# Attention blocks turned through HBM instead of sixteen small transfers, the normalisation moved from GpSimd to VectorE, and a new order of the work

## What is computed

```
x: (128, 128, 256) float32;  adj: (128, 128, 128) int32, 0 or 1, with 1 on the diagonal
nx = layernorm(x; ln1)
q, k, v = nx @ wq + bq, nx @ wk + bk, nx @ wv + bv          # 8 heads of 32
bias   = where(adj > 0, 0.1 * adj * adj, -inf)
attn   = softmax(q k^T / sqrt(32) + bias)                   # (128 graphs, 8 heads, 128, 128)
x1     = x + (attn v) @ wo + bo
out    = x1 + gelu(layernorm(x1; ln2) @ w1 + b1) @ w2 + b2  # hidden width 1024
```

## Time and profile before

| | |
|---|---|
| median of 3 runs | 1980.41 us (1977.6 to 1981.12) |
| the profiled execution | 1975.85 us, its span 1974.1 us |
| busy: TensorE / VectorE / ScalarE / GpSimd | 77% / 59% / 56% / 37% of the span |
| TensorE's mean granted clock | 0.889 |
| DMA moved | 113.29 MB, 57 GB/s on average |
| instructions | 35182 |

### The profile page before, as it was taken

The page is one execution under the profiler, slowest core; times in us unless marked ns, Lnnn a source line. Parts: engine busy times, 40 slices in busy tenths (PEclk is TensorE's granted clock), DMA queues, the critical chain, the costliest instruction groups (busy, mean ns, idle before and its releaser), DMA issues.

```text
span 1974.1 us, 35182 instructions
## 1 busy us (share of the span) xinstructions
PE 1528.4 (77%) x11580; PEld 1288.1 (65%) x11580; DVE 1161.4 (59%) x2130; ACT 1114.1 (56%) x3140; POOL 722.8 (37%) x552
## 2 busy tenths in 40 slices
PE   6468778788778788778788778788778788778777
PEld 5347667667666666667667666667667666666667
DVE  4466656566565566565566565566565566565553
ACT  3355555565555565655565555565555565655542
POOL 4244432244332344332344332344332344332320
PEclk8589888888899898988898898898898898898889
DMA  3222211222112222112222111222112222111110
GB/s 110 57 59 60 58 53 49 62 67 59 51 48 59 63 65 60 53 46 60 63 66 57 53 49 56 64 66 58 53 47 58 64 65 59 52 47 55 49 50 26
DMA packets 153413, 113.29 MB, mean 57 GB/s; under 512 B 36112, under 2 KB 153104, under 8 KB 153360
## 3 DMA queue, kind: packets, MB, share of 16 engines
q1 hardware_dynamic: 153360, 112.61, 20.2%
HBM read 28.58 MB, written 16.78 MB: 23 GB/s over the span
## 4 chain that ended last, share of the span: by engine, by line
SPq 62%; PE 13%; issue 10%; DVE 8%; DMA 3%; POOL 2%; ACT 1%; DVEq 0%; POOLq 0%; ACTq 0%
SPq L299 59%; PE work L354 4%; DMA probt<-wa_raw 3%; PE work L356 3%; PE work L355 3%; DVE wa_raw L793 2%; DVE hid_parts L886 2%; POOL rstd L982 2%; PE work L430 2%; PE area L410 2%; SPq L291 1%; DVE st L821 1%; DVE res L897 1%; SPq L282 1%; SPq L273 1%
## 5 line engine op out<-in xcount | busy, mean ns | idle before, releaser
L588 ACT ACTIVATE soft<-soft,nmax 128x128 f32<-128x128 f32 x1024 | 396.5, 392 | 5.5 <-DVE nmax L773 4.8
L979 POOL TENSOR_TENSOR ve<-mv,eps 128x4 f32<-128x4 f32 x64 | 12.9, 202 | 1038.5 <-DVE mv L830 922.9
L430 PE MATMUL work<-probt,vals 128*32 128x128 f32 x2048 | 108.2, 342 | 302.6 <-DMA probt<-wa_raw 302.5
L354 PE MATMUL work<-w_hi,hid_parts 128*128 128x256 f32 x1024 | 302.6, 296 | 4.0 <-DVE res L897 3.0
L994 POOL TENSOR_TENSOR soft<-soft,rinv 128x1024 f32<-128x1024 f32 x128 | 242.8, 1897 | 157.3 <-DVE rinv L783 157.3
L598 ACT ACTIVATE at_hi<-work 128x256 fp32r<-128x256 f32 x128 | 49.1, 383 | 441.5 <-PE work L430 441.5
L430 PEld LDWEIGHTS work<-probt,vals 128*32 128x32 f32 x2048 | 64.5, 130 | 353.4 <-issue 346.2
L355 PE MATMUL work<-w_lo,hid_parts 128*128 128x256 f32 x1024 | 291.2, 284 | 0.0
L356 PE MATMUL work<-w_hi,hid_parts 128*128 128x256 f32 x1024 | 290.7, 284 | 0.0
L802 DVE TENSOR_TENSOR at_lo<-work,at_hi 128x256 fp32r<-128x256 f32 x128 | 54.0, 422 | 361.1 <-ACT at_hi L598 360.9
L886 DVE TENSOR_TENSOR hid_parts<-late_memory,hid_parts 128x512 fp32r<-128x512 f32 x256 | 223.0, 892 | 69.3 <-ACT hid_parts L656 69.3
(11 more groups left out here) (90 smaller groups left out, 3724.2 us busy)
## 6 DMA issues: line engine op xcount, KB each, us to landing
probt<-wa_raw SPq DMA_DIRECT2D x2048, 32.0 KB, 1.9
xin<-in_x SPq DMA_DIRECT2D x32, 512.0 KB, 3.6
out<-res SPq DMA_DIRECT2D x128, 128.0 KB, 1.8
adj_in<-in_adj SPq DMA_DIRECT2D x32, 256.0 KB, 2.8
res<-in_L_gnn_w SPq DMA_DIRECT2D x1, 1024.0 KB, 10.3
late_memory<-in_L_gnn_w SPq DMA_DIRECT2D x1, 1024.0 KB, 11.9
wa_raw<-in_L_gnn_wq SPq DMA_DIRECT2D x1, 256.0 KB, 3.8
wa_raw<-in_L_gnn_wk SPq DMA_DIRECT2D x1, 256.0 KB, 6.1
```

The source lines that it names most:

```text
L354: pe.matmul(o, lhs_hi, rhs_hi, start=first, stop=False)
L430: mm = pe.matmul(mixed[g * HD:(g + 1) * HD, c * P:(c + 1) * P], vals[:, par, b, c * RPB + g, :], probt[:, b % 2, :, g * DC + c, :], start= ...
L588: a = act.activation(soft[:, b % 2, h, :], soft[:, b % 2, h, :], ACT.Exp, bias=nmax[:, b % 2, h:h + 1], accum_out=rsum[:, b % 2, h:h + 1])
```

## The change

`shuffle` is replaced. `send_blocks` writes a whole turned block (512 KB) to a scratch tensor in HBM in one transfer; `fetch_blocks` waits until that has landed and reads it back in four transfers of 128 KB each, every one to a quarter of the partitions. `normalise` goes from GpSimd to VectorE, with the same operands. The orders of all engines and the banks of `UNITS` are new: `down` 3 lies in the step of the others, `flip` "nt" opens the step of `up`, `mix` 0 lies at the end of the step before the other mixes.

```diff
-LAND = RPB * RPB * 16
+LAND = RPB * 16
-FIRST, EARLY, LATE = -2, 6, 2
+FIRST, EARLY, LATE = -2, 4, 2
+        moved = nc.dram_tensor("moved_blocks", (2, RPB, HD, RPB, BLK), F32, kind="Internal").ap()
...
-            def shuffle(step, off, b):
...
+            def send_blocks(step, off, b):
...
                 sp.wait_ge(blocks_ready, step.through(off, GB, b))
-                for i in range(RPB):
-                    for j in range(RPB):
-                        sp.dma_start(probt[j * HD:(j + 1) * HD, b % 2, i, :, :],
-                                     blocks[i * HD:(i + 1) * HD, b % 2, j, :, :]).then_inc(landed[b % 2], 16)
+                sp.dma_start(moved[b % 2].rearrange("i k j n -> (i k) (j n)"),
+                             blocks[:, b % 2, :, :, :].rearrange("p j h q -> p (j h q)")).then_inc(sent[b % 2], 16)
+
+            def fetch_blocks(step, off, b):
...
+                sp.wait_ge(sent[b % 2], step.through(off, 2, b // 2, 16))
+                for j in range(RPB):
+                    sp.dma_start(probt[j * HD:(j + 1) * HD, b % 2, :, :, :].rearrange("p i h q -> p i (h q)"),
+                                 moved[b % 2, :, :, j, :].rearrange("i k n -> k i n")).then_inc(landed[b % 2], 16)
...
             def body(step):
+                send_blocks(step, -1, 2)
                 load_adj(step, 2)
-                store(step, -3, 3)
-                shuffle(step, -1, 2)
-                shuffle(step, -1, 3)
+                fetch_blocks(step, -1, 2)
+                send_blocks(step, -1, 3)
+                fetch_blocks(step, -1, 3)
                 store(step, -2, 0)
+                send_blocks(step, 0, 0)
+                fetch_blocks(step, 0, 0)
                 store(step, -2, 1)
-                shuffle(step, 0, 0)
+                send_blocks(step, 0, 1)
                 store(step, -2, 2)
                 load_x(step, 2)
-                shuffle(step, 0, 1)
+                store(step, -2, 3)
+                fetch_blocks(step, 0, 1)
...
+            def normalise(step, off, b):
...
+                dve.wait_ge(sum_inverted, step.through(off, GB, b))
+                dve.tensor_tensor(soft[:, b % 2, :, :], soft[:, b % 2, :, :],
+                                  rinv[:, b % 2, :].rearrange("p (h a) -> p h a", a=1).to_broadcast([P, H, P]),
+                                  ALU.mult).then_inc(normed, 1)
```

More of the change, by code:

```diff
@@ L522, in body @@
             def body(step):
[L523 to L525 removed]
+                values(step, 0, 0)
+                flip(step, -2, "nt", 0)
+                flip(step, -2, "nt", 1)
                 score(step, 0, 0)
+                project_out(step, -1, 0)
+                values(step, 0, 1)
+                mix(step, -1, 1)
                 up(step, -2, 0)
[L528 removed]
                 up(step, -2, 1)
[L530 removed]
                 up(step, -2, 2)
                 up(step, -2, 3)
+                project_out(step, -1, 1)
                 up(step, -2, 4)
                 up(step, -2, 5)
[L535 to L536 removed]
                 mix(step, -1, 2)
+                up(step, -2, 6)
+                up(step, -2, 7)
                 score(step, 0, 1)
[L539 removed]
                 project_out(step, -1, 2)
[L541 removed]
+                down(step, -2, 0)
+                flip(step, 1, "xt", 0)
+                flip(step, 1, "xt", 1)
                 mix(step, -1, 3)
[L543 removed]
                 score(step, 0, 2)
+                down(step, -2, 1)
                 project_out(step, -1, 3)
[L546 to L549, removed]
                 down(step, -2, 2)
+                down(step, -2, 3)
+                score(step, 0, 3)
                 query_key(step, 1, 0)
@@ L553, in body @@
                 query_key(step, 1, 2)
-                flip(step, -1, "nt", 0)
-                flip(step, -1, "nt", 1)
-                score(step, 0, 3)
+                mix(step, 0, 0)
+                query_key(step, 1, 3)
             steps(pe, groups, body)
@@ L900, in body @@
             def body(step):
-                add_edges(step, -1, 3)
-                maximum(step, -1, 3)
+                stats1(step, 1)
+                residual(step, -1, 0)
+                flip_lo(step, -2, "nt", 0)
                 flip_lo(step, -2, "nt", 1)
[L904 to L908, removed]
                 invert(step, -1, 3)
-                turn_blocks(step, -1, 2)
+                normalise(step, -1, 3)
@@ L911, in body @@
                 add_edges(step, 0, 0)
+                turn_blocks(step, -1, 3)
+                norm1(step, 1, 0)
+                attn_lo(step, -1, 1)
                 hidden_lo(step, -2, 0)
-                attn_lo(step, -1, 1)
-                turn_blocks(step, -1, 3)
+                maximum(step, 0, 0)
                 hidden_lo(step, -2, 1)
+                norm1(step, 1, 1)
+                residual(step, -1, 1)
+                stats2_of(step, -1, 0)
                 hidden_lo(step, -2, 2)
-                stats2_of(step, -1, 0)
@@ L918, in body @@
[L918 to L921, removed]
+                hidden_lo(step, -2, 3)
+                hidden_lo(step, -2, 4)
                 norm1(step, 1, 2)
+                hidden_lo(step, -2, 5)
                 attn_lo(step, -1, 2)
                 norm1(step, 1, 3)
-                hidden_lo(step, -2, 3)
+                hidden_lo(step, -2, 6)
+                add_edges(step, 0, 1)
+                hidden_lo(step, -2, 7)
@@ L926, in body @@
+                residual(step, -1, 2)
                 stats2_of(step, -1, 1)
[L927 to L930, removed]
+                maximum(step, 0, 1)
+                stats2_of(step, -1, 2)
+                result(step, -2, 0)
+                invert(step, 0, 0)
+                normalise(step, 0, 0)
                 attn_lo(step, -1, 3)
-                maximum(step, 0, 1)
+                turn_blocks(step, 0, 0)
@@ L933, in body @@
+                flip_lo(step, 1, "xt", 0)
+                add_edges(step, 0, 2)
                 residual(step, -1, 3)
-                stats2_of(step, -1, 2)
-                hidden_lo(step, -2, 6)
-                hidden_lo(step, -2, 7)
+                flip_lo(step, 1, "xt", 1)
                 stats2_of(step, -1, 3)
+                invert(step, 0, 1)
+                maximum(step, 0, 2)
                 stats2(step, -1)
-                invert(step, 0, 0)
-                flip_lo(step, 1, "xt", 0)
+                result(step, -2, 1)
@@ L941, in body @@
+                normalise(step, 0, 1)
                 norm2(step, -1, 0)
-                result(step, -2, 0)
-                result(step, -2, 1)
+                turn_blocks(step, 0, 1)
+                result(step, -2, 2)
+                add_edges(step, 0, 3)
+                result(step, -2, 3)
+                invert(step, 0, 2)
                 norm2(step, -1, 1)
-                invert(step, 0, 1)
-                flip_lo(step, 1, "xt", 1)
-                turn_blocks(step, 0, 0)
                 norm2(step, -1, 2)
-                result(step, -2, 2)
@@ L950, in body @@
-                add_edges(step, 0, 2)
-                maximum(step, 0, 2)
+                maximum(step, 0, 3)
+                normalise(step, 0, 2)
                 norm2(step, -1, 3)
-                turn_blocks(step, 0, 1)
-                flip_lo(step, -1, "nt", 0)
+                attn_lo(step, 0, 0)
+                turn_blocks(step, 0, 2)
                 if not step.steady and step.n == 0:
```

55 lines of the change are left out of this document (23 added, 32 removed), and 3 rows, old and new, of the table UNITS.

## The result

The changed kernel takes 1496.07 us (median of 4 runs, 1492.71 to 1498.11) against 1979.01 for the kernel before (4 runs): ratio 0.7558, 95% interval 0.7541 to 0.7575. The forecast was 1531 us with a range of 1440 to 1650. The profiled execution took 1498.11 us, its span 1496.3.

A forecast was written before the change was run, and what follows sets the result against it. The kernel before was taken as bound by a ring of late blocks behind SP's small DMAs, 59.3 us a step. Forecast: 31 steps of 45.3 us plus ends of 55.7 and 69, span 1529, so 1531 us; range 1440 to 1650.

The forecast's parts named there:

- The ring of late blocks: Kernel before, 59.3 us a step: SP issues blocks late, the mix waits 9.5 us a step, delaying results and stores.
- Transfers: SP's queue: 4 sends and 16 fetches replace 64 issues a step; a block lands after 8.4 us, before 11.9.
- Normalise: Four operations move from GpSimd to VectorE at 1.22 us each: VectorE at 41.4 us a step, GpSimd at 15.0.
- Rival C: VectorE becomes the bound, its normalises held up by GpSimd: 49.0 us a step, 1645 us; chance 0.21.
- the forecast's tail: VectorE's last third of a step: norm2 0 loses 2.4 us beside residual_start, making query_key 1 1.6 us late.
- The walk: One steady step followed through the four new engine orders: 43.2 us plus 2.1 of lateness, 45.3 us a step.
- the other way: VectorE starts norm2 0 ahead of GpSimd, nothing is late, TensorE alone bounds: 43.2 us a step, 1465 us; chance 0.23.
- the floor: TensorE's own work a step, added up from start-to-start times: 42.2 us, before 1.0 us of waiting at values 0.
- semaphore hops: TensorE at query_key 1 and 2: an estimated 0.5 us a step added to the 1.6 us of lateness.
- The ends: Outside the steady steps: 55.7 us before the first load_x unchanged, 69 behind the last whole steps in place of 78.8.
- The tail: End of the run, behind the last two whole steps: 69 us in place of 78.8.
- The signs named ahead: Profile after: SP under 15% of chain, VectorE and TensorE above 88% busy, clock above 0.97, one norm2 in four at 2.4.

The follow-up runs named there:

- experiment 2: Kernel before, its order and GpSimd normalise kept, with send_blocks and fetch_blocks back to back in place of each shuffle: 1583.73 us, ratio 0.8001.
- experiment 5: New order with the sixteen small transfers a block again, and load_x moved ahead of block 1's shuffle on SP's queue: 1627.26 us, ratio 0.8226.
- experiment 6: Changed kernel with each block written to HBM twice, the second write issued after the first has landed: 1498.49 us, ratio 0.7575.
- experiment 8: Changed kernel with result 2 and result 3 taken ahead of norm2 0 on VectorE: 1458.99 us, ratio 0.737.
- experiment 10: Changed kernel with residual_start ahead of the second rstd, results 2 and 3 ahead of norm2 0, and query_key 3 in bank 1: 1408.98 us, ratio 0.7115.
- experiment 7: Changed kernel with residual_start moved ahead of the second rstd (rstd_of_n) in GpSimd's list: 1435.04 us, ratio 0.7247.
- experiment 9: Changed kernel with query_key 3 written to bank 1 in place of bank 0: 1475.97 us, ratio 0.7453.

## Why the forecast was right, step by step

*What bounds before.* The ring of late blocks is confirmed, with two additions. Of the 12.3 us a step of TensorE's waiting in the steady steps the blocks were 8.7 and 3.6 were the flip's (experiment 2), which the forecast's reading left out though its new order removes it. And the transfers alone take 395 us off the old order and 256 off the new one with GpSimd's normalise (1766 to 1510); the new order alone takes 213 off, but 74 with the transfers in HBM (1584 to 1510). Both make late blocks come in time, so their gains don't add; and the 213 are kept down by the new order's own fault, the load of x behind a shuffle. The forecast's words, no pure queue bound but a ring, hold: experiment 5 has all of the small transfers' issuing and runs 48.25 us a step against 59.3. Two parts were not run by themselves: VectorE's normalise in the old order, and EARLY at 4 in place of 6.

*Transfers.* 8.4 us a block were forecast, 7.2 came: the send lands after 2.6 (taken as 3.6) and is issued in 0.34; a fetch is issued in 0.43 (taken as 0.6) and lands after 2.8 (taken as 1.8). The two landings were each 1.0 us wrong, in opposite directions, and cancel by luck. The slack would have made either error harmless, as experiment 6 shows.

*Normalise.* VectorE at 41.4 was forecast, 40.3 came. Some of that is errors that cancel: a normalise takes 1.389 us on average in place of 1.22 and `norm2` 1183 ns in place of 797, but `hidden_lo` takes 683 in place of 892, since `result_start` no longer falls beside it, which the forecast did not count. GpSimd was put at 15.0 and is busy 16.6, with its `pow` held. Rival C, VectorE as the bound, is out: experiment 8 gains 37 us with its work unchanged, and in experiment 10 the step is TensorE's floor. The cost lies in what stands behind the held instruction, not in the sum of the holds.

The Trainium skill's rule ("SBUF — State Buffer", "Who interferes with whom": two SBUF inputs against a reading GpSimd instruction, an exclusive lock) agrees with this case's trace at `normalise` 3: 1.93 us in the change, and 3.19 in experiment 8, where it ends 1.08 us after `result_start`. The `pow` at 1.96 us in place of 1.04 is the same the other way round. `norm2`, on which the forecast's tail rests, has only one such input, and the rule as cited doesn't cover it; that it is held too is shown by the runs alone (2.48 us, and 0.41 when `residual_start` is moved away).

*The walk.* `query_key` 1 was to come 1.6 us late for want of `result` 2 and waits 1.56; `norm2` 0 was to lose 2.4 us in a collision and loses 2.1 (2.48 against 0.40); `values` 0 was to wait 1.0, and shows 0.85 of idle time and 1.02 from start to start. Experiments 7, 8 and 9 take away the collision or a wait, and the time comes back. The forecast saw that the start of `residual_start` beside `norm2` 0 would decide it, a matter of 0.06 us here, and gave the other way a chance of 0.23. The term that was mis-sized is the floor, 0.6 too high (42.2 against 41.6). For the 0.5 us of semaphore hops no row was given; what the starts show beyond the idle time at `query_key` 1 and 2 is 1.92 − 1.56 = 0.4, of about that size, but that it is hops isn't shown. Together 45.3 against 44.5 us a step, 25 us over 31 steps.

*The ends.* Here a step of the forecast failed, if by little: nothing before the first `load_x` was said to get shorter, and it went out at 48.5 in place of 55.7. Its old place in the queue was behind a shuffle that held the queue from 45.5 to 55.6 us, as the timeline of the kernel before had it; in the new one it follows a send that takes 0.34. The tail was put at 69 and is 1496.3 − 48.5 − 31 × 44.5 = 68. So 8 of the 33 us between forecast span and measured span are the ends, the rest the step.

*The signs named ahead.* Clock above 0.97: 0.98 over the span. SP under 15% of the chain: 0%. TensorE above 88%: 92%; VectorE 87%, just short. One `norm2` in four at 2.4 or more: yes, but the others, up to 1.4 us, lie beside `edges` and are longer too; the mean is 1183 ns in place of 804.

## What to carry to other kernels

Walk one steady step of a pipelined kernel with the trace's start-to-start times, engine by engine: here it named both of the waits that were left, to within 0.2 us, and each was then removed by moving a line or a bank number. In a queue of many small issues look at what stands behind them, not only at what they carry: one load moved ahead of sixteen transfers was worth 115 us. And judge a load on a nearly full engine by which waiting instruction stands behind it: with normalise on VectorE it was busy 3.6 us a step more and the kernel was 14 us faster, while 2 us in front of one result cost 31 times 2. Count a short wait of TensorE from start to start: 1.56 us of idle time were 1.9.

## What the runs showed of the hardware that was not expected

- A write of 512 KB from SBUF to HBM landed after 2.6 us, sooner than a read of the same size (3.6 before and 4.5 after, with the DMA engines 39% busy in place of 20%; whether that is the cause wasn't tested). A read of 128 KB into 32 partitions took 2.8, a store of 128 KB from 128 partitions 1.8 before and 2.3 after.
- SP's issue times in three forms: 0.34 us for 512 KB in one piece per partition, 0.43 for 128 KB in 1 KB pieces, 0.63 from start to start for 32 KB from SBUF to SBUF.
- GpSimd is held too: its `pow` on 128 x 4 elements took 1.04 us alone and 1.96 beside VectorE's normalise, and in experiment 7 `residual_start`, beside `normalise` 3, took 3.18 to 3.27 in place of 2.38.
